# Attention of a Macaron block written out step by step: row maxima by block transpose, head sums by ones columns, outputs turned through DRAM

## The reference

```
x = x + 0.5 * ffn(layernorm(x))
x = x + attn(layernorm(x))
x = x + 0.5 * ffn(layernorm(x))
```

## Time and profile before

| what | value |
|---|---|
| median of 3 runs | 894.6 us (891.29 to 894.69) |
| the profiled execution | 889.24 us, of it the span 887.4 us |
| mean granted TensorE clock | 0.953 of full speed |
| TensorE busy | 794.1 us, 89% |
| VectorE busy | 772.9 us, 87% |
| ScalarE busy | 606.2 us, 68% |
| GpSimd busy | 112.1 us, 13% |
| chain that ended last | PE 57%, ACT 17%, issue 13%, DVE 8%, POOL 3% |
| the reduction of the scan, L689 | 512 of them, mean 1219 ns |
| the exponential, L887 | 1024 of them, mean 605 ns |

### The profile page before, as it was taken

How to read it: one execution, slowest core, us unless ns; L and a number is a source line. 1 busy time by engine, 2 the same in 40 slices (tenths; PEclk the granted TensorE clock), 3 DMA queues, 4 the chain that set the end, 5 groups by cost and what they waited for, 6 DMA issues and landing times.

```text
span 887.4 us, 16511 instructions
## 1 busy us (share of the span) xinstructions
PE 794.1 (89%) x5207; PEld 271.5 (31%) x5207; DVE 772.9 (87%) x1043; ACT 606.2 (68%) x1144; POOL 112.1 (13%) x273
## 2 busy tenths in 40 slices
PE   5876679999999998999999899999999999998885
PEld 3654431222222222222222222222222222223364
DVE  6889988899999997999999889999999999984376
ACT  2214751788888886888778778888888888884611
POOL 3344330000000000001000000000000000001023
PEclk9997885999999998999999999999999999998999
DMA  4000010000000000000000000000000000000001
GB/s 101 1 1 0 0 48 1 7 7 8 8 7 8 8 8 9 8 7 7 8 7 7 10 8 7 7 8 13 8 8 1 1 2 1 2 1 1 1 12 36
DMA packets 8239, 8.72 MB, mean 10 GB/s; under 512 B 2784, under 2 KB 6496, under 8 KB 8160
## 3 DMA queue, kind: packets, MB, share of 16 engines
q0 software_dynamic: 1536, 4.20, 1.3%
q1 hardware_dynamic: 4272, 2.82, 1.1%
q10 hardware_dynamic: 2352, 0.66, 0.4%
HBM read 2.23 MB, written 1.05 MB: 4 GB/s over the span
## 4 chain that ended last, share of the span: by engine, by line
PE 57%; ACT 17%; issue 13%; DVE 8%; POOL 3%; ACTq 1%; DVEq 0%; DMA 0%; POOLq 0%; SPq 0%
PE ps L1095 25%; PE ps L1084 21%; ACT ring L887 15%; PE ps L1069 4%; PE ps L1112 4%; ACT outT L895 2%; DVE mh L689 2%; POOL XB L341 1%; PE ps L942 1%; DVE xn L461 1%; DVE X L647 1%; DVE terms L642 1%; DVE ring L637 1%; PE ps L1140 1%; ACTq L886 1%
## 5 line engine op out<-in xcount | busy, mean ns | idle before, releaser
L887 ACT ACTIVATE ring<-ps 128x512 f32<-128x512 f32 x1024 | 532.6, 605 | 163.8 <-PE ps L1084 162.1
L689 DVE TENSOR_REDUCE mh<-ps 128x1 f32<-128x1024 f32 x512 | 603.1, 1219 | 38.0 <-PE ps L1069 25.3
L1069 PE MATMUL ps<-KT,QS 48*128 48x512 bf16 x1024 | 354.7, 396 | 3.4 <-DVE mh L689 2.5
L1084 PE MATMUL ps<-QS,KT 51*128 51x512 bf16 x1024 | 314.9, 390 | 33.0 <-ACT ring L887 20.6
L1095 PE MATMUL ps<-ring,Vx 128*32 128x512 f32 x2048 | 276.7, 613 | 2.6
L1084 PEld LDWEIGHTS ps<-QS,KT 51*128 51x128 bf16 x1024 | 76.1, 94 | 334.3 <-ACT ring L887 294.3
L1069 PEld LDWEIGHTS ps<-KT,QS 48*128 48x128 bf16 x1024 | 75.6, 94 | 84.0 <-DVE mh L689 60.1
L409 POOL TENSOR_TENSOR mp<-zeros,top 128x8 bf16<-128x8 f32 x32 | 6.2, 194 | 470.1 <-DVE top L699 470.1
L1095 PEld LDWEIGHTS ps<-ring,Vx 128*32 128x32 f32 x2048 | 40.6, 108 | 64.6 <-issue 49.9
L829 ACT ACTIVATE ring<-ps 128x512 f32<-128x512 f32 x32 | 17.2, 602 | 45.7 <-DVE ring L524 25.3
L418 POOL DMA_DIRECT2D QS<-QT x32 | 18.1, 567 | 154.3 <-PE ps L1084 154.3
(11 more groups left out here) (110 smaller groups left out, 385.9 us busy)
## 6 DMA issues: line engine op xcount, KB each, us to landing
QS<-QT POOLq DMA_DIRECT2D x32, 128.0 KB, 2.0
QS<-mrow SPq DMA_DIRECT2D x64, 3.0 KB
out_dram<-X SPq DMA_DIRECT2D x4, 256.0 KB, 2.3
wfc_n<-in_L_ffn_W_fc_dram SPq DMA_DIRECT2D x1, 256.0 KB, 3.1
wpj_n<-in_L_ffn_W_proj_dram SPq DMA_DIRECT2D x1, 256.0 KB, 3.6
rope<-rope_tables ACTq DMA_DIRECT2D x1, 128.0 KB, 6.2
w_n<-in_L_attn_wq_dram ACTq DMA_DIRECT2D x1, 64.0 KB, 3.4
w_n<-in_L_attn_wk_dram ACTq DMA_DIRECT2D x1, 64.0 KB, 6.6
```

Source lines behind the costliest of these rows:

```text
L689: v.tensor_reduce(mh[:, n // A_STEP % 2, at:at + 1], ps[:, slot_banks(s), :].rearrange("p a b -> p (a b)"), AX.X, ALU.max).then_inc(a_free, 1)
L887: a.activation(ring[:, k % PRING, :], ps[:, EXP[k % C_EXP], :], ACT.Exp, scale=SCALE)\
L1069: mm = t.matmul(ps[:, A0 + 2 * (s % 2) + x, :], QS[rows, j, q * P:(q + 1) * P], KT[rows, j, (2 * half + x) * 512:(2 * half + x + 1) * 512] ...
L1084: t.matmul(ps[:, EXP[n % C_EXP], :], KT[rows, j, kt * P:(kt + 1) * P], QS[rows, j, :], start=True, stop=True).then_inc(b_ready, 1)
```

## The change

- **No loops in the attention.** All 32 steps are written out on all five engines, with constants in every wait.
- **No shared slot.** The transpose of mp, the four pick matmuls, the copy, the reciprocals of 128 x 8 and the product of 128 x 64 are gone from the steps.
- **Maxima.** VectorE turns mp (now 128 x 32) in blocks of 32 x 32 (max_rows), two units into the next step. Four DMAs of SP for head 0 and four of GpSimd for head 1 put 12 rows of 32 numbers each into the three spare rows of QT itself. QS and the copies into it (load_q) are gone; both kinds of matmul read QT.
- **Head sums.** Vx has 8 columns of v and 8 of ones for each head (VW = 16), so PO holds 8 equal rows of sums. The copy of PO goes to DRAM after every step (sums_out, 256 KB). Once in a chunk eight DMAs (sums_in) bring it back with the heads' rows on 128 partitions, GpSimd adds the two halves (add_sums, 2 operations of 128 x 512), VectorE takes 128 x 512 reciprocals, GpSimd multiplies (divide). The result is already turned, so "T" in late() is gone; wo's rows are permuted to match (wo_n, one copy at the start).
- **Lead.** LEAD is 25 instead of 23.
- **The end.** For chunks 0 to 2, "O" and "F" still stand between batches of the last two steps. Chunk 3's round trip through DRAM runs beside the second feed-forward part of chunks 0 to 2, which is written out; chunk 3 is projected after contract and sum_squares of chunk 1 and normalized after those of chunk 2. Normalized rows have a place for each chunk (xl), and residual sums for chunks 0 to 2 are made ahead.

The diff, cut to its core:

```diff
-VW = HD + 1
+VW = 2 * HD
...
-LEAD = 23
+LEAD = 25
...
+    sums = nc.dram_tensor("head_sums", [NG, P, CS], F32, kind="Internal").ap()
...
+        def row_slots(h, j, c, a):
+            to = QT[HR * h + R_QK:HR * h + R_ALL, j, c * CS:(c + 1) * CS]
+            return to.rearrange("r (q a n) -> r q a n", q=CT, a=4)[:, :, a, :]
...
+            def rows(g):
+                j, c = g % PAIRS, g // PAIRS
+                sp.wait_ge(rows_ready, g + 1)
+                for a in range(4):
+                    sp.dma_start(row_slots(0, j, c, a), mrow[32 * a:32 * a + 3 * CT, g % 2, :])\
+                        .then_inc(m_in[0][j], 16)
+            def sums_out(g):
+                sp.wait_ge(po_free, g + C_ONE + 1)
+                sp.dma_start(sums[g], outT[:, g % 2, :]).then_inc(o_out[g % 2], 16)
+            def sums_in(c):
+                for x in range(2):
+                    sp.wait_ge(o_out[x], 16 * (c + 1) * PAIRS // 2)
+                if c:
+                    sp.wait_ge(ot_ready, c)
                 for h in range(2):
-                    dst = QS[HR * h + R_QK:HR * h + R_ALL, j, :].rearrange("r (q n) -> r q n", q=CT)
-                    sp.dma_start(dst, mrow[h * 3 * CT:(h + 1) * 3 * CT, i % 2, :]).then_inc(m_in[j], 16)
-            rows(0, 0)
-            with sp.Fori(0, NC - 1) as c:
-                for i in range(1, PAIRS + 1):
-                    rows(i, c)
-            for i in range(1, PAIRS):
-                rows(i, NC - 1)
-            with sp.Fori(0, NC) as c:
...
+            def rows(i):
+                j, c = i % PAIRS, i // PAIRS
+                pool.wait_ge(rows_ready, i + 1)
+                for a in range(4):
+                    g.dma_start(row_slots(1, j, c, a), mrow[32 * a + 3 * CT:32 * a + 6 * CT, i % 2, :])\
+                        .then_inc(m_in[1][j], 16)
+            def add_sums(c):
+                pool.wait_ge(od_in, 16 * OD_DMAS * (c + 1))
+                g.tensor_tensor(OD[:, 2, :], OD[:, 2, :], OD[:, 3, :], ALU.add).then_inc(od_sum, 1)
+                g.tensor_tensor(OD[:, 0, :], OD[:, 0, :], OD[:, 1, :], ALU.add).then_inc(od_sum, 1)
+            def divide(c):
+                pool.wait_ge(od_sum, 2 * (c + 1))
+                pool.wait_ge(od_rec, c + 1)
+                g.tensor_tensor(OT[:, c * CS:(c + 1) * CS], OD[:, 0, :], OD[:, 3, :], ALU.mult).then_inc(ot_ready, 1)
+            pool.wait_ge(t_ev, C_EXP + TURNS * NC)
+            for i in range(NG):
+                cut_max(i)
+                rows(i)
+                if i >= PAIRS and i % PAIRS == SUM_AT:
+                    add_sums(i // PAIRS - 1)
+                if i >= PAIRS and i % PAIRS == SUM_AT + 1:
+                    divide(i // PAIRS - 1)
+            for c in range(NC - 1):
                 ln_scale(2, c, c)
-            ffn(1)
+                residual(1, c)
+            hidden_scale(1, 0)
+            add_sums(NC - 1)
+            divide(NC - 1)
+            hidden_scale(1, 1)
+            ln_scale(2, NC - 1, NC - 1)
...
+            def max_rows(i):
+                dve.wait_ge(mp_ready, i + 1)
+                if i >= 2:
+                    for h in range(2):
+                        dve.wait_ge(m_in[h][(i - 2) % PAIRS], 16 * ROW_DMAS * ((i - 2) // PAIRS + 1))
+                v.transpose(mrow[:, i % 2, :], mp[:, i % 2, :]).then_inc(rows_ready, 1)
+            def reciprocals(c):
+                dve.wait_ge(od_sum, 2 * (c + 1))
+                v.reciprocal(OD[:, 3, :], OD[:, 2, :]).then_inc(od_rec, 1)
+            for n in range(UNITS):
+                row_max(n)
+                g, u = n // A_STEP, n % A_STEP
+                if u == A_STEP - 1:
+                    whole_max(g)
+                if g and u == CUT_AT - 1:
+                    max_rows(g - 1)
+                if g > PAIRS and g % PAIRS == SUM_AT + 1 and u == REC_AT:
+                    reciprocals(g // PAIRS - 1)
+            max_rows(NG - 1)
...
+            for c in range(NC - 1):
+                output_chunk(c)
+            dve.wait_ge(b_ready, (NG - 4) * B_STEP)
+            for c in range(NC - 1):
+                norm_rows(2, X2, c, c)
+                if c:
+                    take(c - 1)
+            take(NC - 2)
+            squares(1, 0)
+            chunk_and_next(1, 0, 0)
+            reciprocals(NC - 1)
+            chunk_and_next(1, 1, 1)
+            output_chunk(NC - 1)
+            variance(1, 2, 0)
+            norm_rows(2, X2, NC - 1, NC - 1)
+            update(1, 2, 0)
+            take(NC - 1)
+            squares(1, NC - 1)
+            variance(1, NC - 1, 1)
+            update(1, NC - 1, 1)
         @block.scalar
...
+            def take_out(g):
+                act.wait_ge(pv_done, (g + 1) * NB + C_RING)
+                if g >= 2:
+                    act.wait_ge(o_out[g % 2], 16 * (g // 2))
+                a.copy(outT[:, g % 2, :], ps[:, PO, :]).then_inc(po_free, 1)
+            for g in range(NG):
+                for k in range(B_STEP):
+                    exp_tile(g, k)
+                    if g and k == OUT_AT:
+                        take_out(g - 1)
+            take_out(NG - 1)
...
+            def exp_mm(g, k):
                 b, r4 = k // BATCH, k % BATCH
                 h, kt = r4 // 2, 2 * b + r4 % 2
-                n, j = i * B_STEP + k, i % PAIRS
+                n, j, c = g * B_STEP + k, g % PAIRS, g // PAIRS
+                rows = slice(HR * h, HR * h + R_ALL)
                 if k == 0:
-                    pe.wait_ge(m_in[j], (c + i // PAIRS + 1) * 32)
-                pe.wait_ge(p_ready, c * B_IT + n + (C_EXP if n == SPLIT else 1))
-                rows = slice(HR * h, HR * h + R_ALL)
-                t.matmul(ps[:, EXP[n % C_EXP], :], KT[rows, j, kt * P:(kt + 1) * P], QS[rows, j, :],
+                    for h in range(2):
+                        pe.wait_ge(m_in[h][j], (c + 1) * 16 * ROW_DMAS)
...
-            def shared(w, c, last=False):
-                s = shared_slot(w, last)
-                if not last or w < PAIRS - 1:
-                    pe.wait_ge(mp_ready, c * PAIRS + w + 2)
-                slot_free(s, c)
-                if not last or w < PAIRS - 1:
-                    mm = t.transpose(psb[0:2 * 3 * CT, A0 + 2 * (s % 2) + 1, 0:P], mp[:, (w + 1) % 2, :],
-                                     identb[:, :])
-                if type(c) is not int or w > 0 or last:
-                    pe.wait_ge(po_free, c * PAIRS + w + C_ONE)
-                    for q in range(CT):
-                        mm = t.matmul(ps[:, A0 + 2 * (s % 2), q * 2 * VW:(q + 1) * 2 * VW],
-                                      outT[:, (w - 1) % 2, q * P:(q + 1) * P], pick[:, :], start=True, stop=True)
...
+            for g in range(NG):
+                for k in range(B_STEP):
+                    n = g * B_STEP + k
+                    exp_mm(g, k)
+                    if n + 2 * LEAD < 2 * UNITS:
+                        max_mm(n + 2 * LEAD)
+                    if k % BATCH == BATCH - 1:
+                        b = n // BATCH - 1
+                        if b >= 0:
+                            pv_batch(b // NB, b % NB)
+                        if (g, k // BATCH) in LATE:
+                            late(*LATE[g, k // BATCH])
+            pv_batch(NG - 1, NB - 1)
+            pe.wait_ge(taken, NC - 1)
+            expand(1, 0)
+            pe.wait_ge(p_ready, NG * B_STEP + C_EXP)
+            pe.wait_ge(po_free, NG + C_ONE)
             expand(1, 1)
-            late("F", 3)
-            ffn(1)
+            both(1, 0, 0)
+            expand(1, 2)
+            both(1, 1, 1)
+            late("O", NC - 1)
+            both(1, 2, 0)
+            late("F", NC - 1)
+            pe.wait_ge(taken, NC)
+            expand(1, 3)
+            both(1, 3, 1)
```

More of the change, by code:

```diff
@@ new lines, in _ @@
+            rows(0)
+            for g in range(NG):
+                if g:
+                    sums_out(g - 1)
+                if g + 1 < NG:
+                    rows(g + 1)
+                if g and g % PAIRS == 0:
+                    sums_in(g // PAIRS - 1)
+            sums_out(NG - 1)
+            sums_in(NC - 1)
+            for c in range(NC):
+                sp.wait_ge(y_ready, c + 1)
+                sp.dma_start(out.rearrange("a (t p) d -> p (a t) d", p=P)[:, c * CT:(c + 1) * CT, :],
@@ L314, in _ @@
                             pattern=[[-1, P]], channel_multiplier=1)
-            for par in range(2):
-                g.affine_select(out=pick[:, :].rearrange("p (h n) -> p h n", h=2),
-                                in_=pick[:, :].rearrange("p (h n) -> p h n", h=2),
-                                compare_op=ALU.not_equal, fill=1.0, base=-32 * par,
-                                pattern=[[-64, 2], [-1, VW]], channel_multiplier=1).then_inc(ident0, 1)
-                pool.wait_ge(ident0, par + 2)
             g.memset(half_neg[:, :], -0.5)
@@ L364, in _ @@
             pool.wait_ge(setup_v, SETUP_V)
-            ffn(0)
+            with pool.Fori(0, NC - 1) as c:
+                residual(0, c)
```

(65 more changed lines are left out.)

386 lines of the change are left out of this document (133 added, 253 removed).

## The result

The median went from 892.94 us to 863.29 us (four runs each; after 857.98 to 865.9): a ratio of 0.966, 95% interval 0.961 to 0.972. The forecast was 840 us with a range of 824 to 866. The direction was right and the forecast gain too large: 29.7 us came of some 53. The median also lies outside the narrower range of 826 to 850 us in which the forecast itself was to hold. The profiled execution took 857.98 us, 21 us over the 837 us of the sum.

What follows compares the result with a forecast made beforehand. Attention was bound by a 2.39 us ring of TensorE and ScalarE per batch, plus the shared slot. 889.2 - 58.4 + 1.0 + 6.5 + 2.15 + 1.5 - 5 = 837 us profiled, so 840 us forecast, range 824 to 866.

Steps and rivals of the forecast that it cites:

- Slot and loop: Attention steps: without shared slot and loops a step lasts 19.3 us; 36.3, 6.2, 1.5 and 8.8 us go.
- The late work: Last two attention steps: the T pieces go, three O and three F stay at 4.9 us; gain 5.6 us with the slot.
- Maxima and rows: Each step: block transpose 0.2 us on VectorE; row DMAs land in 4.8 to 6.8 of 7 us, nothing charged.
- the 1 us charged to VectorE's delays: Attention steps: two VectorE delays under 0.39 us, charged 0.03 us a step, 1 us in all.
- just inside: Head of a step: row DMAs land 4.8 to 6.8 us after the transpose, with 7 us until TensorE needs them.
- The rival of late rows: Heads of steps: eight small DMAs land later than TensorE needs them; 1000 us at a 10 us landing; chance 0.08.
- VectorE as the bound: Rival, attention: reductions run at 1.22 us instead of 1.13, a step is 19.9 us, total 859; chance 0.12.
- Reciprocals: Three of 128 x 512 within the scan: 2.5 us each, 0.35 hidden, 6.5 us lost in all (+28 / -6).
- The end: Last product to the end: 46 us instead of 50.9, a gain of 5 us, with 42 to 56.
- Lead and start: Before the first exponential: two more lead units +2.15 us, larger Vx fill and start +1.5 us (0 to 5).
- the rivals of 852 to 859 us: VectorE bound 859 (0.12), waits not what made loops slow 857 (0.10), end or reciprocals dearer 852 (0.09).
- the end or the reciprocals cost more: Rival: reciprocals at eight passes, or chunk 3's round trip 8 us late: 852 us; chance 0.09.

Runs made afterwards that it cites:

- the small ones: Kernel after the change, with the three reciprocals within the scan cut to 8 of 512 columns: 843.87 us, ratio 0.947.
- all three edits: Kernel after the change, with all row DMAs by SP, reciprocals in eight pieces and chunk 3's sums earlier: 840.31 us, again 837.11 us.

## Why the prediction was right in direction and too large

*Slot and loop, right.* The step was to be 19.3 us and is 19.34, the batch 2.39. Both parts are shown on their own: 0.54 us a step and 8.8 us at the returns by the old kernel without loops, 0.95 us a step by the slot put back (TensorE's four matmuls alone). 53 us of the forecast rest on this. The late work in the last two steps was to cost 4.9 us and costs 2.9 (steps of 22.55 and 19.01 us).

*Maxima and rows, right.* Nothing of them appears in a plain step. The transpose takes 0.20 us, 7.7 us are in hand where 7 were forecast, and the 1 us charged to VectorE's delays doesn't appear. With two units less in hand, some steps grow; so "just inside" was the right reading. One source was read too widely: the landing of 2.0 us is that of GpSimd's 128 KB copies alone, as SP's DMAs have none in the trace. The rival of late rows falls, and so does VectorE as the bound: it still has its 1.13 us a reduction (4.64 us for four).

*Reciprocals, mis-sized.* The forecast had 2.5 us each and 2.15 of loss, 6.5 in all. The reciprocal takes 3.34 us, and the three steps lose 4.65, 5.19 and 5.41, 15.3 in all. Two things were wrong. By the forecast's own rule (duration less 0.35 us) the longer reciprocal alone makes it 3.0 us a time, 2.5 more in all. The other 6.3 us are a second cost that the term left out, though the prediction itself used it in the rival of late rows: after a stop TensorE comes back at the lower clock and loses another 2 us or so. That the whole comes with the reciprocals is shown by the small ones, which lose nothing.

The duration can be read from three sizes now: 193 ns for 8 columns, 544 for 64, 3344 for 512. They lie on 0.14 us and 6.25 ns a column. The forecast had the fixed part right and took 4.9 ns a column, from a difference of 39 ns over 8 columns. The Trainium skill ("VectorE: DVE Perf Modes", on the resources of a lane) gives the divide a repeat count of 8, from which 4.6 us was estimated (8 times 1.13 / 1024 us for each of 512 columns is 4.5). The measured 3.34 us lies between that and 2.5, so the count of 8 at the rate of reductions is too high here.

*The end, mis-sized and one part not seen.* The stretch from the last product to the end was to be 46 us (bound 48.4) and was 61.0.
- The gelus of chunks 0 to 2 came 2.0, 10.8 and 19.2 us after T, as worked out (2.8, 11.2, 19.6). Chunk 3's came at 39.1, not 35.2. The sum for this stretch left out the reciprocal of 3.35 us on VectorE; TensorE stands 3.87 us before the projection, and the windows of 815 to 835 us have granted clocks of 0.83 and 0.73. Taking the reciprocal ahead won 2.2 us.
- From there to the sums of squares 8.0 us, not 5.9.
- So 48.4 + 3.9 + 2.1 = 54.4 us behind T, about where SP reaches its own drain (849.9, so T + 54.7). Then SP waits 6.1 us at the closing barrier, because GpSimd's drain takes 11.6 us. The prediction counted the issues added to GpSimd, not what they leave to its end. Without them (all row DMAs by SP) the drain is 1.12 us and this stretch 5.3 us shorter.

*Lead and start, right within about 1 us* in the profiled execution: +2.5 against +3.65. The lead of 23 shows the parts: with it the first exponential matmul is at 151.0 us, as before. So the two units cost 2.5 us (2.15 forecast) and the start nothing (1.5 forecast), though the larger fill of Vx took 3.72 us, as worked out.

But the median of after is 5.3 us above its profiled execution. One kernel, that with all three edits, was profiled twice: with a granted clock of 0.65 in the window of 118 to 152 us its first exponential matmul is at 153.6 us, with 0.50 at 158.5, and the stretch from there to T is 627.8 us both times. After's profiled execution had 0.65. Its mean clock over the whole span was 0.947, that of its three longer executions 0.932 to 0.935. So it is likely that these three had the lower clock at the start of attention; without their traces that isn't shown.

*How the forecast came out within its range.* The sum missed by 21 us, and 840 us were forecast. The range reached up to 866 us and so took in the rivals of 852 to 859 us, of which only "the end or the reciprocals cost more" (0.09) came true, and by both at once: reciprocals +8.8 us, end +15.1. The table's middle row nearly closes: 8.8 for the reciprocals and 1.2 for 0.04 us more in each step, less 1.0 for VectorE's delays and 2.0 for the late work, is 7.0 of 7.1 us. That the median still fell inside is in part the width of the range.

*Open:* how much of the end is the lower clock and how much the order of the work; no run separates them.

## What to carry to other kernels

Price a long operation put ahead of the queue that feeds TensorE as stop plus restart: one of 3.34 us cost 5.1 here, and the same work in eight pieces 0.4 (four steps at 0.1), as long as the input of the first piece is there. When a change gives an engine DMAs to issue, follow that engine to the end of the program, not only past the issues. A slack must be measured, too: the rows had 7.7 us and needed more than 5.3. In the last 50 us, where each chunk depends on another, every added operation needs its place in the sum. And where executions of one kernel differ by more than the effect, compare stages of the traces, not only medians.

## What the hardware showed beside that

- GpSimd's drain at the end grew with the DMAs it had issued in the program: 1.12 us with none, 3.75 with 32 (the kernel before), 11.6 with 128. That is 0.082 us for each DMA, by (3.75 - 1.12) / 32 and by (11.6 - 1.12) / 128. Three counts lie on a line; why is not shown.
- The reciprocal of fp32 takes 6.25 ns a column and 0.14 us beside that: 3.34 us for 512 columns, 0.54 for 64, 0.19 for 8.
- After each of the three stops of 2.25 us TensorE had a mean granted clock of 0.53 to 0.57 for about 7 us.
- Ahead of the first exponential (118 to 152 us), the same instructions ran at a mean granted clock of 0.50 in one execution and 0.65 in another.
